# A longer ring of gathered rows, queries kept in DRAM, and buffers that share the ring's place: one graph block on one core

## The chip, the cores and the metric

The kernel runs on one core of one Trainium2 chip. The metric is device time of one launch in microseconds (us). TensorE is the matrix engine (PE in the profile, PEld its weight loads), VectorE is DVE, ScalarE is ACT, GpSimd is POOL, and SyncE is SP; SPq, ACTq and POOLq are the queues on which engines issue DMAs and other instructions that are not counted as busy.

## The reference

One block of a graph network on N = 3125 nodes of D = 256 features with 50000 edges, all in float32. `dst` is sorted and thickest at low node numbers.

```python
dst = (3125 * uniform(50000) ** 2).astype(int)          # sorted; src uniform
xn = layernorm(x)
# 1. graph attention, 8 heads; every node also has an edge to itself
h = einsum('nf,hfd->hnd', xn, W)
e = leaky_relu(a_s[:, src] + a_d[:, dst], 0.2)
alpha = segment_softmax(e, dst)                          # for each head
agg = sum_h softmax(gate)[h] * segment_sum(h[src] * alpha, dst)
g = layernorm(agg + gate @ bias + xn) @ Wo.T + bo
# 2. linear attention over all nodes, 8 heads of 32
q, k, v = rmsnorm(xn) @ w_qkv;  q = elu(q) + 1;  k = elu(k) + 1
o = (q @ (k.T @ v)) / (q @ k.sum(0) + eps)
m = xn + o @ w_out + b_out;  m = m + rmsnorm(m)
x = x + g + m
# 3. mixture of 16 experts, two for each node
x = x + layernorm(xn2 + sum_of_two w_k * expert_k(xn2)),  xn2 = layernorm(x)
```

## The kernel before

The program is four blocks, one after the other; all engines meet between two blocks.

**First stage** (0 to 142 us). Tables for the edges are made, then a software pipeline (`pipeline`, with a lag for each part) goes over NT = 25 tiles of 128 nodes. For tile t, VectorE normalises x; ScalarE copies it to `xna` and copies its transpose (`copies`); TensorE multiplies with w_qkv; ScalarE takes exponentials (`exps`); VectorE forms q and k (`elu`) and writes the source scores `a_s` beside the node's row; TensorE adds k.T v and transposes q; ScalarE copies that transpose to `qT` in SBUF (`qTs`, lag 3, line 393). SP waits for `a_sb` and stores the tile as rows of 272 words in `node_rows` in DRAM (`store`, line 315), and at tiles 7 to 11 also one fifth of `flag_rows` (`store_flags`, line 321). Last it stores `ad_rows` (line 324).

**Edge stage** (142 to 798 us). The 50000 edges, in falling order of `dst`, are cut into 391 chunks of 128; nodes are taken in windows of 16. A step is a chunk met with a window: 592 steps in 37 groups of 16. GpSimd gathers the 128 source rows of each chunk (139 KB) from `node_rows` into a slot of the ring `rows` with an indirect DMA (line 738), in order of chunks:

```python
for k in range(CHUNKS):
    if k >= len(s_rows):                  # FLY = 4 in flight
        landed(k - len(s_rows))           # waits, then raises `fetched`
    if k >= FLY:
        pool.wait_ge(prod.sem, free_at[k])
    pool.indirect_dma_start(rows[:, k % RING, :], ...)
# free_at[k] = max(1, ends[k-FLY] + 2 + AHEAD*G - LEAD,
#                     ends[k-RING] + 2 + AHEAD*G  if k >= RING)
```

`ends[k]` is the last step that uses chunk k, and `prod` counts the products done, from 33 when the first begins. So a gather may start LEAD = 48 steps before the chunk four earlier is used up, and not before the slot's last user is done (RING = 40). For group g, ScalarE waits until `fetched` has reached the group's last chunk and copies the source scores of its 16 steps (`copy_as`, line 917); TensorE turns them to scores (`scores`, line 999) in its turn g + 1, in which it does the products of group g - 1; segment maxima and exponentials follow on VectorE and ScalarE; VectorE spreads the weights over the windows (`spread`, line 819, two of 8 steps) and TensorE multiplies them with the gathered rows (`product`, line 1048) in its turn g + 2. VectorE adds each product to a running sum (`accumulate`, line 835), and SP stores these sums to `agg_rows` in quarters of 8 steps (line 1134).

In the same groups, for g below 25, one tile of linear attention is finished: TensorE multiplies the tile's queries with `kvd` (`num`, line 1058), VectorE adds and inverts the sum (`z_sum`, `z_inverse`) and divides (`divide`), TensorE turns and projects (`turn`, `out_proj`, lines 1065 to 1074). On TensorE `num(0)` stands ahead of group 0's masks, and `out_proj(0)` ahead of `scores(0)`; on VectorE `z_sum`, then `mask_eq` and `bias_parts`, then the inverse, `divide` and `mask_ad`, which needs `adsd`. SP loads `adsd` (line 1123) from `ad_step` before the groups begin, and in them first the flags (line 1127).

**Node stage** (798 to about 1150 us). For each tile the node's own sum is gathered, multiplied with W, added to the residual x2, normalised and sent to its experts' rows.

**Expert stage** (to the end). 64 tiles of 128 rows go through two layers; then each node gathers its two results.

## Time and profile before

| what | value |
|---|---|
| time, median of 3 runs | 1491.21 us (1490.78 to 1492.29) |
| span of the profiled execution | 1489.6 us |
| TensorE busy | 1175.3 us, 79% |
| VectorE busy | 996.3 us, 67% |
| ScalarE busy | 499.2 us, 34% |
| GpSimd busy | 692.2 us, 46% |
| mean granted TensorE clock | 0.887 of 2.4 GHz |
| DMA, mean over the span | 172 GB/s |

Durations below come from the one profiled execution, whose span is 1.6 us below the median of the runs. A granted clock of 1.00 is 2.4 GHz and 0.50 is 1.2 GHz. Busy shares over the whole span mix stages with different limits; the windows by stage are read instead. In a timeline, brackets give how long the engine was idle before the instruction and what released it.

### The profile page before, as it was taken

How to read it: one execution, taken by the hardware profiler on the slowest of the kernel's cores; microseconds unless marked ns; L12 is line 12 of the kernel's file. 1: busy time of each engine (PE TensorE's matmuls, PEld its weight loads, DVE VectorE, ACT ScalarE, POOL GpSimd, SP SyncE). 2: the span in 40 equal slices, each digit the busy share in tenths (PEclk: the TensorE clock that was granted, in tenths of full speed). 3: DMA queues.
4: the chain of work that ended last, by engine and by line, in shares of the span. 5: the costliest groups of instructions: out<-in, count | busy, mean ns of one | idle time of the engine just before them, and what ended most of it. 6: DMA issues, size and time to landing. Idle time of an engine off the chain costs nothing. (4 is left out here: it accounts for less than half of the span.)

```text
span 1489.6 us, 30544 instructions
## 1 busy us (share of the span) xinstructions
PE 1175.3 (79%) x6192; PEld 946.9 (64%) x6193; DVE 996.3 (67%) x2854; ACT 499.2 (34%) x1969; POOL 692.2 (46%) x782
## 2 busy tenths in 40 slices
PE   4996699999999878666672799999991799999900
PEld 4664466666666656444451688888881689999800
DVE  6565388888888867665674588899965234444378
ACT  2453233333333322221121655555521123333301
POOL 1001765666666566666621457676753011111175
PEclk9898599999999998787795799999995799999955
DMA  6062678888888777676757534334413972222155
GB/s 194 30 109 78 142 238 247 238 240 249 249 253 246 234 221 224 207 213 197 222 149 218 195 125 135 127 134 139 143 53 129 343 257 70 70 70 70 61 166 179
DMA packets 219212, 255.70 MB, mean 172 GB/s; under 512 B 57205, under 2 KB 193016, under 8 KB 215640
## 3 DMA queue, kind: packets, MB, share of 16 engines
q1 hardware_dynamic: 177464, 140.79, 30.0%
q0 software_dynamic: 30992, 103.79, 24.1%
q10 hardware_dynamic: 10640, 9.86, 2.1%
q8 instruction: 38, 0.62, 0.2%
q14 instruction: 78, 0.64, 0.1%
HBM read 139.69 MB, written 114.67 MB: 171 GB/s over the span
## 5 line engine op out<-in xcount | busy, mean ns | idle before, releaser
L738 POOL DMA_INDIRECT rows<-node_rows,srcT x391 | 389.0, 995 | 217.5 <-PE pO L1048 107.6
L1048 PE MATMUL pO<-rows,pw 128*128 x1184 | 337.2, 416 | 33.5 <-DVE pw L819 29.4
L835 DVE SCALAR_TENSOR_TENSOR acc<-acc,rsc,pO 128x257 f32<-128x257 f32 x592 | 281.0, 475 | 60.2 <-PE pO L1048 29.9
L1048 PEld LDWEIGHTS pO<-rows,pw 128*128 128x128 f32 x1184 | 216.5, 202 | 78.7 <-issue 51.7
L1408 PE MATMUL pW_<-W_again,aT 128*128 128x256 f32 x800 | 183.1, 383 | 0.4 <-DVE res L1476 0.4
L1408 PEld LDWEIGHTS pW_<-W_again,aT 128*128 128x128 f32 x800 | 149.8, 192 | 19.5 <-DVE res L1476 0.7
L1854 POOL DMA_DIRECT2D ys_rows<-ye x64 | 34.5, 539 | 238.0 <-DVE ye L1805 238.0
L1744 ACT ACTIVATE hT<-pHe,b 128x128 f32<-128x128 f32 x256 | 73.0, 368 | 192.8 <-PE pHe L1770 174.8
L1770 PEld LDWEIGHTS pHe<-xeT,w1e 128*128 128x128 f32 x1024 | 127.4, 196 | 13.7 <-DVE w1e L1795 10.5
L1770 PE MATMUL pHe<-xeT,w1e 128*128 128x128 f32 x1024 | 128.1, 279 | 9.9 <-DVE xeT L1788 9.9
L1779 PE MATMUL pYe<-w,hT 128*128 x512 | 122.1, 382 | 1.2 <-issue 0.6
L1460 DVE SCALAR_TENSOR_TENSOR own<-AG,al,own 128x256 f32<-128x256 f32 x200 | 108.4, 556 | 7.3 <-ACT own L1342 3.6
L917 ACT ACTIVATE asb<-rows 128x8 f32 x592 | 72.9, 209 | 106.2 <-POOLq L729 95.7
L1779 PEld LDWEIGHTS pYe<-w,hT 128*128 128x128 f32 x512 | 92.9, 192 | 12.3 <-issue 2.2
L819 DVE TENSOR_TENSOR pw<-pexp,eq 128x1024 f32<-128x1024 f32 x74 | 87.2, 1220 | 0.0
L1795 DVE COPY w1e<-w 128x1024 f32 x64 | 44.4, 694 | 63.6 <-issue 38.4
L1342 ACT ACTIVATE own<-xna,al 128x256 f32 (+1 forms) x200 | 82.2, 499 | 3.6 <-DVEq L1588 3.6
L1397 PE MATMUL pa<-cst,own 128*128 128x128 f32 x400 | 52.7, 289 | 37.1 <-DVE own L1460 37.1
L1788 DVE COPY xeT<-pXe 128x256 f32<-128x256 f32 x64 | 27.2, 424 | 78.2 <-PE pXe L1760 78.2
L1397 PEld LDWEIGHTS pa<-cst,own 128*128 128x128 f32 x400 | 48.0, 151 | 38.8 <-issue 34.4
L1315 POOL DMA_INDIRECT xs_rows<-ysc,slot_x x50 | 50.9, 1019 | 23.8 <-DVE slot_x L1568 10.3
L1863 POOL DMA_INDIRECT w1e<-ys_rows,slot x50 | 48.8, 976 | 17.2 <-issue 13.4
(332 smaller groups left out, 1929.1 us busy)
## 6 DMA issues: line engine op xcount, KB each, us to landing
agg_rows<-acc SPq DMA_DIRECT2D x296, 256.0 KB
w<-in_ffn_w SPq DMA_DIRECT2D x32, 512.0 KB, 5.8
xe<-xs_rows ACTq DMA_DIRECT2D x64, 128.0 KB, 2.0
ys_rows<-ye POOLq DMA_DIRECT2D x64, 128.0 KB, 2.0
rows<-node_rows,srcT POOLq DMA_INDIRECT x391
node_rows<-xna SPq DMA_DIRECT2D x25, 136.0 KB, 1.8
xna<-in_x SPq DMA_DIRECT2D x5, 640.0 KB, 11.2
mix_rows<-hx SPq DMA_DIRECT2D x25, 128.0 KB
```

The costliest lines, as they stand in the source:

```text
L738: pool.indirect_dma_start(rows[:, k % RING, :], None, node_rows[:, :], at_row(srcT[:, k:k + 1])).then_inc(s_rows[k % len(s_rows)], 16)
L819: dve.tensor_tensor(pw[:, i, :, :].rearrange("p s (d h) -> p s d h", h=H), pexp[:, g % V2, s, :].unsqueeze(2).to_broadcast([P, HG, DW, H]) ...
L835: dve.scalar_tensor_tensor(out=acc[:, k % V3, s % HG, 0:D + 1], in0=before, scalar=rsc[:, g % V2, s:s + 1], in1=pO[n % PB][:, 0:D + 1], op ...
L917: ins = act.activation(asb[:, g % V2, s, :], rows[:, ds(at[s], 1), AS:AS + H].rearrange("p c h -> p (c h)"), ACT.Copy)
L1048: pe.matmul(pO[n % PB][:, 0:D + 1], pw[:, s // HG, s % HG, :], rows[:, ds(at[s % 4], 1), 0:D + 1].rearrange("p c f -> p (c f)"), start=Tru ...
L1342: ins = act.activation(own[:, c, h, :], tile(xna, t, 0, D), ACT.Copy, scale=al[:, 1, t, h:h + 1] if isinstance(t, int) else al[:, 1, ds(t, ...
L1397: mm = pe.transpose(pA[i][:, k * P:(k + 1) * P], own[:, c, n // KD, (n % KD) * P:(n % KD + 1) * P], ident)
L1408: mm = pe.matmul(pW[:, 0:D], aT[:, c, n, :], W[:, n % KD, n // KD, :], start=(n == 0), stop=(n == H * KD - 1))
L1460: ins = dve.scalar_tensor_tensor(out=own[:, c, h, :], in0=AG[:, c, h, :], scalar=al[:, 0, t, h:h + 1] if isinstance(t, int) else al[:, 0, ...
L1744: ins = act.activation(hT[:, c % 2, f, :], pH[c % 2][:, f * P:(f + 1) * P], ACT.Relu, bias=b1[:, ds(e, 1), f:f + 1].rearrange("p e f -> p ...
L1770: mm = pe.matmul(pH[c % 2][:, f * P:(f + 1) * P], w1e[:, c % S3, k, f * P:(f + 1) * P], xeT[:, c % 2, k, :], start=(k == 0), stop=(k == KD ...
L1779: mm = pe.matmul(pY[c % 2][:, 0:D], hT[:, c % 2, f, :], of_expert(w2, e, f), start=(f == 0), stop=(f == FK - 1))
```

## The change

- The ring has 63 slots instead of 40, and a gather may start 96 steps ahead instead of 48.
- Queries of linear attention no longer stay in SBUF. In the first stage ScalarE copies them to one of two buffers `qTo`, after the store of the tile two earlier has landed; SP stores them to DRAM (`store_q`) three turns behind the tile's rows. In the edge stage SP loads tile g + 1 in group g (`load_q`), tile 0 before the groups, and TensorE waits for it in `num`.
- The ring is allocated first and for the whole program. W and WT of the first stage lie in it, and later `y_all`, `x2`, the second W, `b2` and the buffers of the expert stage.
- The semaphores `al_done`, `m_in` and `a_rt` are gone; `al_in` and `al_ex` count on instead.

```diff
-RING, FLY, LEAD, AHEAD = 40, 4, 48, 2
+RING, FLY, LEAD, AHEAD = 63, 4, 96, 2
...
-        both_y = sb("qT_y", [P, NT * D])
-        qT = both_y.rearrange("p (k n) -> p k n", k=KD)
-        y_all = both_y.rearrange("p (t f) -> p t f", f=D)
+        ring = sb("ring", [P, RING * RW])
+        rows = ring.rearrange("p (r f) -> p r f", f=RW)
+
+        def part(lo, *shape):
+
+            n = math.prod(shape)
+            names = "abcd"[:len(shape)]
+            sizes = dict(zip(names, shape))
+            return ring[:, lo:lo + n].rearrange(f"p ({' '.join(names)}) -> p {' '.join(names)}", **sizes)
+
+        Y_END = NT * D
+        y_all = part(0, NT, D)
+        q_rows = dram("q_rows", (NT, P, D))
...
-            W = sb("W", [P, KD, H, D], ctx=ctx)
+            W = part(0, KD, H, D)
...
-            WT = sb("WT", [P, KD, H, KD, P], ctx=ctx)
+            WT = ring[:, KD * H * D:2 * KD * H * D].rearrange("p (k h d n) -> p k h d n", h=H, d=KD, n=P)
+            qTo = sb("qTo", [P, 2, KD, P], ctx=ctx)
+            s_q = [sem(f"s_q{c}") for c in range(2)]
...
-                    pipeline(sp, NT, [(0, store), (0, store_flags)], extra=12)
+                    def store_q(t, c, r):
+                        wait(sp, qT_sb, t)
+                        out_q = q_rows[t, :, :] if isinstance(t, int) else q_rows[ds(t, 1), :, :].rearrange("t p f -> (t p) f")
+                        sp.dma_start(out_q, qTo[:, c, :, :].rearrange("p k f -> p (k f)")).then_inc(s_q[c], 16)
+                    pipeline(sp, NT, [(3, store_q), (0, store), (0, store_flags)], extra=9)
+                    for c in range(2):
+                        sp.wait_ge(s_q[c], 16 * len(range(c, NT, 2)))
                     sp.dma_start(ad_rows.rearrange("(t p) h -> p t h", p=P), ad[:, :, :]).then_inc(moves.sem, 16)
...
                     def qTs(t, c, r):
                         wait(act, qT_ps, t)
-                        act.activation(qT[:, :, t * P:(t + 1) * P] if isinstance(t, int) else qT[:, :, ds(t * P, P)],
-                                       pq[:, 0:D].rearrange("p (k f) -> p k f", k=KD), ACT.Copy).then_inc(qT_sb.sem, 1)
+                        if not isinstance(t, int) or t >= 2:
+                            act.wait_ge(s_q[c], r * 16)
+                        act.sem_inc(s_gate, 1)
+                        act.activation(qTo[:, c, :, :], pq[:, 0:D].rearrange("p (k f) -> p k f", k=KD), ACT.Copy).then_inc(qT_sb.sem, 1)
...
-            rows = sb("rows", [P, RING, RW], ctx=ctx)
+            qTb = sb("qTb", [P, 2, KD, P], ctx=ctx)
+            q_stored = [16 * len(range(c, NT, 2)) for c in range(2)]
...
                     def num(t):
                         wait(pe, mixed, t - 1)
+                        pe.wait_ge(s_q[t % 2], q_stored[t % 2] + 16 * (t // 2 + 1))
                         for g in range(KD):
-                            mm = pe.matmul(pX[:, g * (P + 4):(g + 1) * (P + 4)], qT[:, g, t * P:(t + 1) * P], kvd[:, g, :], start=True, stop=True)
+                            mm = pe.matmul(pX[:, g * (P + 4):(g + 1) * (P + 4)], qTb[:, t % 2, g, :], kvd[:, g, :], start=True, stop=True)
...
-                    groups([(0, load_flags), (2, load_tops), (1, store_x2), (2, store(0)), (1, store_top), (2, store(1))])
+                    def load_q(t):
+                        if t < NT:
+                            wait(sp, num_ps, t - 2)
+                            sp.dma_start(qTb[:, t % 2, :, :].rearrange("p k f -> p (k f)"), q_rows[t, :, :]).then_inc(s_q[t % 2], 16)
+
+                    def load_next_q(g):
+                        load_q(g + 1)
+                    load_q(0)
+                    groups([(0, load_next_q), (0, load_flags), (2, load_tops), (1, store_x2), (2, store(0)), (1, store_top), (2, store(1))])
...
-        W = sb("W_again", [P, KD, H, D], ctx=node_ctx)
-        x2 = sb("x2", [P, NT, D], ctx=node_ctx)
+        x2 = part(Y_END, NT, D)
+        W = part(2 * Y_END, KD, H, D)
...
-                    act.wait_ge(al_done, 1)
+                    act.wait_ge(al_in, 2)
...
-        b2 = sb("b2", [P, E, D], ctx=experts_ctx)
+        b2 = part(Y_END, E, D)
```

## Rows read from the trace of the kernel before

**Rows 1.** Windows: us, busy of PE, PEld, DVE, ACT, POOL; clock, DMA share, GB/s

```profile
210.00:509.00 299.00, 278.72 (x1385) 202.36 (x1384) 256.94 (x702) 105.85 (x600) 185.05 (x183) 1.00 0.82 245
509.00:776.00 267.00, 190.31 (x789) 135.89 (x787) 174.54 (x438) 62.44 (x372) 163.01 (x167) 0.82 0.70 208
```

**Rows 2.** Waits, 509 to 776 us: us in total, times, longest

```profile
ACT asb L917 <- POOLq L729: 65.3, 13, 9.9
...
PE pM L999 <- ACT asb L917: 36.8, 10, 7.3
```

**Rows 3.** Timeline of VectorE, line 819 (start, duration) of groups 1, 21, 35 and 36

```profile
196.14 2.35 DVE L819 TENSOR_TENSOR pw<-pexp,eq 128x1024 f32<-128x1024 f32 x2
...
494.36 2.35 DVE L819 TENSOR_TENSOR pw<-pexp,eq 128x1024 f32<-128x1024 f32 x2
...
761.23 2.35 DVE L819 TENSOR_TENSOR pw<-pexp,eq 128x1024 f32<-128x1024 f32 x2
...
775.07 2.35 DVE L819 TENSOR_TENSOR pw<-pexp,eq 128x1024 f32<-128x1024 f32 x2
```

**Rows 4.** Line 738, whole span: durations, first and last start; its idle time

```profile
L738 POOL DMA_INDIRECT rows<-node_rows,srcT x391: 940/946/1987, 149.3 to 754.6; - x196
...
  PE pO L1048: 107.6, 154
...
  DMA rows<-node_rows,srcT: 23.7, 29
```

**Rows 5.** Window of line 738 alone, its first 45 us: busy, clock, DMA share

```profile
149.00:194.00 45.00, 31.05 (x32) 0.60 0.66 154
```

**Rows 6.** Timeline of ScalarE: the last copy at line 917

```profile
761.68 1.95 ACT L917 ACTIVATE asb<-rows 128x8 f32 x16 [1.64 <-issue]
```

**Rows 7.** Timeline of the first stage, one tile and the next exponential

```profile
60.05 0.69 ACT L378 ACTIVATE ez<-pQ,rr 128x512 f32<-128x512 f32 x1 [1.60 <-PE pV L443]
...
62.56 10.90 SPq L315 DMA_DIRECT2D node_rows<-xna  x4
...
64.66 0.39 ACT L393 ACTIVATE qT_y<-pq 128x256 f32 x1
...
67.10 0.69 ACT L378 ACTIVATE ez<-pQ,rr 128x512 f32<-128x512 f32 x1 [1.46 <-PE pV L443]
```

**Rows 8.** DMA issues: count, KB each, us to landing (6.3: the one at 87.2)

```profile
node_rows<-xna SPq DMA_DIRECT2D x25, 136.0 KB, 1.8
...
flag_rows<-flags SPq DMA_DIRECT2D x5, 516.0 KB, 6.7
...
adsd<-ad_step SPq DMA_DIRECT2D x1, 320.0 KB, 9.8
...
ad_rows<-ad SPq DMA_DIRECT2D x1, 100.0 KB, 4.2
...
node_rows<-xna SPq DMA_DIRECT2D x1, 136.0 KB, 6.3
```

**Rows 9.** A window of 1 us of TensorE, right behind an idle stretch

```profile
134.00:135.00 1.00, 1.00 (x6) 0.50 0.40 139
```

**Rows 10.** Timeline, the end of the first stage

```profile
134.72 0.38 ACT L393 ACTIVATE qT_y<-pq 128x256 f32<-128x256 f32 x1 [2.33 <-PE pq L458]
...
140.96 0.83 DVE L621 SCALAR_TENSOR_TENSOR stepT<-stepT,firstT 128x640 f32<-128x640 f32 x1
```

**Rows 11.** Timeline, the start of the edge stage

```profile
150.07 1.22 PE L1058 MATMUL pMix<-kvd,qT_y 128*128 128x132 f32 x4 [12.03 <-DMA mix_bo<-in_mix_b_out]
...
154.98 8.45 SPq L1127 DMA_DIRECT2D flg<-flag_rows  x2
...
162.19 1.22 PE L1074 MATMUL pMix<-xna,cst 128*128 128x256 f32 x2
...
164.35 0.29 DVE L762 TENSOR_TENSOR adb<-cst,adsd 128x128 f32<-128x128 f32 x1 [6.53 <-DMA adsd<-ad_step]
...
166.74 0.77 PE L999 MATMUL pM<-cst,asb 128*128 128x128 f32 x2 [3.33 <-ACT asb L917]
```

More of the change, by code:

```diff
@@ L18 @@
+import math
 from contextlib import ExitStack
@@ L1173, in build @@
             md_win = dram("md_win", (2 * P * DW, 2 * H))
-            s_mdw, al_in, al_ex, al_done, scale_in = sem("s_mdw"), sem("al_in"), sem("al_ex"), sem("al_done"), sem("scale_in")
+            s_mdw, al_in, al_ex, scale_in = sem("s_mdw"), sem("al_in"), sem("al_ex"), sem("scale_in")
             lr = sb("lr", [P, 2], U32, ctx)
@@ L1185, in build @@
             te = sb("te", [P, 3, E], ctx=ctx)
-            a_rt, m_in, free_in, zero_in = sem("a_rt"), sem("m_in"), sem("free_in"), sem("zero_in")
+            free_in, zero_in = sem("free_in"), sem("zero_in")
             cleared = sem("b2_in")
@@ L1383, in _ @@
                     clear(act, 1)
-                    act.wait_ge(m_in, 1)
-                    act.activation(m[:, 0, :], m[:, 0, :], ACT.Exp).then_inc(a_rt, 1)
+                    act.wait_ge(al_in, 3)
+                    act.activation(m[:, 0, :], m[:, 0, :], ACT.Exp).then_inc(al_ex, 1)
                 @block.tensor
@@ L1587, in _ @@
                         line.do(dve.tensor_tensor(al[:, i, :, :], es[:, 1, :, :], es[:, 2 + i, :, :], ALU.mult))
-                    dve.sem_inc(al_done, 1)
+                    dve.sem_inc(al_in, 1)
                     PICK, L = [(7, top(i)) for i in range(10)], [(8, place(i)) for i in range(5)]
@@ L1626, in _ @@
                     line.do(dve.tensor_scalar(slot[:, :, :].rearrange("p k t -> p t k"), sy[:, :, :], float(SLOTS - 1), None, ALU.min))
-                    dve.tensor_tensor(m[:, 0, :], picks[:, :, 2 * E + 3], picks[:, :, 2 * E + 2], ALU.subtract).then_inc(m_in, 1)
-                    dve.wait_ge(a_rt, 1)
+                    dve.tensor_tensor(m[:, 0, :], picks[:, :, 2 * E + 3], picks[:, :, 2 * E + 2], ALU.subtract).then_inc(al_in, 1)
+                    dve.wait_ge(al_ex, 2)
                     line.do(dve.tensor_scalar(m[:, 1, :], m[:, 0, :], 1.0, None, ALU.add))
@@ L1649, in build @@
             S3 = 3
-            xe = sb("xe", [P, S3, D], ctx=ctx)
-            xeT = sb("xeT", [P, 2, KD, P], ctx=ctx)
-            w1e = sb("w1e", [P, S3, KD, F], ctx=ctx)
-            hT = sb("hT", [P, 2, FK, P], ctx=ctx)
-            ye = sb("ye", [P, 2, D], ctx=ctx)
+            at = Y_END + E * D
+            w1e = part(at, S3, KD, F)
+            at += S3 * KD * F
+            hT = part(at, 2, FK, P)
+            at += 2 * FK * P
+            xe = part(at, S3, D)
+            at += S3 * D
+            xeT = part(at, 2, KD, P)
+            at += 2 * KD * P
+            ye = part(at, 2, D)
+            at += 2 * D
+            xb = part(at, 2, D)
             pX = [ps(ctx, f"pXe{c}") for c in range(2)]
@@ L1678, in build @@
             g = flat_w1[:, 0:VU * 2 * D].rearrange("p (u k f) -> p u k f", k=2, f=D)
-            xb = sb("xb", [P, 2, D], ctx=ctx)
             v = flat_w1[:, VU * 2 * D:VU * 3 * D].rearrange("p (u f) -> p u f", f=D)
```

## The prediction

> **What bounds the kernel now.** I read the windows by stage first. From 210 to 509 us TensorE is busy 279 of 299 us at full clock; from 509 to 776 us it is busy only 190 of 267 us, DMA is less used than before, and the mean granted clock is 0.82 [rows 1]. The reader is to see that the edge stage falls into two halves, and that the second is short of something. The waits of that half say of what: ScalarE waits 65.3 us at line 917 for GpSimd's count of landed gathers, and TensorE then waits 36.8 us for that copy [rows 2]. The timeline of VectorE's line 819, which opens each of the 37 groups, gives the pace: groups 1 to 21 take (494.36 - 196.14)/20 = 14.91 us each. At that pace group 36 would open 15 groups later at 718; it opens at 775.07. The last two groups, for which all rows were there, are 13.84 us apart, since the node work in the group (25 tiles) is over [rows 3].
>
> Is it the gathers' own speed, or when they may start? GpSimd's row answers: 391 gathers from 149.3 to 754.6, at least 0.94 us each, and 154 of them waited for a matmul at line 1048, 107.6 us in all [rows 4]. That is free_at: 48 steps ahead, or slot free. In the first half a chunk is used for nearly 2 steps (windows are met along with chunks), so 48 steps are some 27 chunks; toward the end a chunk lasts 1 step (0.93 us) and a gather takes longer than that. What GpSimd stood still for in the first half is missing in the second. Of 48 steps some 30 are needed anyway, because the copy at line 917 runs two groups ahead of the products.
>
> **The ring (63 slots, 96 steps).** A wait that is met at once still shows 0.3 us of idleness, so the true wait is 107.6 - 154 x 0.3 = 61.4 us [rows 4]. Would the new bounds hold a gather? From the formula of dst, chunk k ends near step s(k) = k + 195 (1 - (1 - k/391)^2). With the chain going on at 1.4 us a gather, gather 184 starts 258 us after the first, and its step bound, s(180) - 96 = 222 steps of 0.93 us after products begin at 181 (one group before 196.14), is passed 20 us earlier; gather 243 needs slot s(180) = 318, passed 12 us earlier; gather 390 needs s(327) = 517, over 25 us earlier. So the waits on products vanish and the chain lasts 605.3 - 61.4 = 543.9 us, 1.395 us a gather. The first 45 us, in which no bound holds it, show the same: 32 gathers, 1.41 us each [rows 5].
>
> Against that, waits for landings (only four gathers may be in flight) partly hid behind the waits on products, and DMA, at a share of 0.82 in the first half [rows 1], carries a tenth more a microsecond. Bounds: nothing added (1.395), or 1.50 a gather, at which two thirds of the gain is gone. The rows are nearer to the first (the second half, short of gathers, is less loaded than the first), so I take 12 us, 0.03 a gather. Removed: 61.4 - 12 = 49.4 us. The last copy began 7 us after the last gather started, held by ScalarE's order and not by the landing [rows 6]; now it follows the landing by perhaps 5 us, 2 us more. From the copy to group 36's opening is 13.4 us as now [rows 3, 6]. Everything from there to the end is unchanged in work.
>
> The Trainium skill (DMA: Bandwidth & Descriptors, Queues, rings and completion order) says that each DMA engine takes packets from its queue rows in turn. By it the gathers, on a row of their own, would not slow with SP's load, and the 12 us would be nought. No row of before shows the chain free and the load full at once.
>
> **Queries stored (first stage).** Per tile SP issues one more DMA (25 of 128 KB), and ScalarE, before it copies tile t's queries, waits for the store of t - 2. SP gets to store_q(t) only after store(t + 2). The loop turns in 3.52 us. From the exponential at 60.05 to SP's issue of that tile's rows is 2.51 us; from the query copy at 64.66 to the next exponential 2.44 us, of which 1.46 idle, so 0.98 of work [rows 7]. Two tiles, 7.04 us, must hold 2.51 + 0.4 (SP's issue) + landing + 0.1 + 0.98, so the landing may take 3.0 us. Node rows, 136 KB, take 1.8 us [rows 8]: hidden, with 1.2 us left. If that cover goes, each microsecond above 3.0 costs one per two tiles.
>
> It goes at tiles 7 to 11, where SP also stores the flags: 516 KB in small packets, 6.7 us to land, and node rows issued 3 us behind one take 6.3 us, so the queue is served in order [rows 8]. The query store comes right behind: a landing 0.4 + 6.7 + 0.8 after SP's store, a two-tile cycle of 2.51 + 7.9 + 0.1 + 0.98 = 11.5 instead of 7.04. Queued behind the waiting ScalarE copy are the next tile's x copies and exponentials, for which VectorE and TensorE wait. Five flag stores stand in three such cycles: 3 x 4.4 = 13 us. Slower tiles thin the backlog (less, 9), and a TensorE that has stood idle comes back at half clock [rows 9] (more, up to 18). I take 13. The other end is nought, if ScalarE had as much air as it has elsewhere; the rows for the flags exclude it.
>
> At the stage's end ad_rows now follows the last query store: the copy at 134.72 + 0.38, SP 0.1, 1.8 to land, ad_rows 4.2 to land [rows 8]: 141.2, and VectorE works until 141.8 [rows 10]. Nothing, or 0.5 us if it fails.
>
> **Queries loaded (edge stage).** 25 loads, each a group ahead of its use: hidden by a 15 us group. Not the first. load_q(0) stands on SP behind adsd, which takes 9.8 us to land [rows 8]; SP's next two issues there took 8.45 us, so the queue is full. VectorE sees adsd at 164.35; the queries land near 165.2 instead of being in place at 150.07. The line-1058 matmul, z_sum, the bias work, division and projection take 150.07 to 163.41, which adsd covered; all of it moves by 15.1 us, to 178.5, and the scores of group 0 behind it on TensorE from 166.74 to 178.5: 11.8 us [rows 11]. Who is late? Products, not gathers, and the gathers are what sets the end. So I cost it at nothing, covered by the gather chain; uncovered it is 11.8 us.
>
> **Layout and semaphores.** W, WT, y_all, x2, b2 and the expert buffers lie in the ring, al_done, m_in and a_rt are merged into counters in the same order: same instructions, same order, nothing. A buffer's address costs nothing that a row shows.
>
> **Sum.** 1489.6 + 13 - 49.4 - 2 = 1451.2; the runs' median lies 1.6 above the profiled 1489.6, so 1452.8, 1453.
>
> **Check from the consumer.** Without lack of rows group 36 opens at 494.36 + 3 x 14.91 + 12 x 13.84 = 705, plus 13 and 11.8: 730. The sum has it at 775.1 - 38.4 = 736.7. The gathers still bound, by 7 us only, so cheaper gathers can give no more than 7 us beyond the sum.
>
> **Rivals.** (a) The consumer bounds: gathers at 1.395 or less, or the flag slips nearer to 9. Both together give 1442. For it: the two clocks of the check lie close. Chance 0.17. (b) Gathers slow under load to about 1.48: 0.055 x 390 = 21 us more than mine, 1474. For it, the landing waits that were hidden; against it, the first 45 us. Chance 0.15. (c) Slower than before: the wait at landed(k - 4), with four in flight, takes the place of the wait for products. Each gather at g gives a sum of 1453 + 390 (g - 1.426); it decides from g = 1.53, where a landing would take 4 x 1.53 = 6.1 us on average. At 1.60 the time is 1521. Rows show only 29 such waits among 391, none on the average gather. Chance 0.10. (d) The change of the ring does nothing, because gathers are bound by DMA anyway: then only 13 us are added, 1504. Against it the 61.4 us of waits on products, which are no DMA. Chance 0.03. (e) About no change, between (b) and (c): 0.03. My forecast has 0.52.
>
> **Range.** 1438 takes in (a) with the flags at 9 and VectorE's tail groups faster than 13.84; 1486 takes in (b) with flags at 18 and part of (e). Beyond lie (c) and (d). Measurement can tell 0.2% (3 us) from no change. Faster 0.84, same 0.03, slower 0.13.
>
> **What would show it.** Right: GpSimd's waits on line 1048 nearly gone, last gather about 36 us earlier, no wait of ScalarE at line 917 before 600 us; group 36 opening near 737; a gap of TensorE of some 4 us three times between 75 and 105 us; line 1058 first at 165 plus the first stage's delay. Wrong: landing waits on most gathers; ScalarE waiting on stores in every tile of the first stage; SP's stores of acc late enough that VectorE waits for them.

## The result, and the profile after

The changed kernel takes 1497.89 us (median of 9 runs, 1492.69 to 1501.47), the kernel before 1491.62 us on the same chip (median of 9 runs, 1488.63 to 1493.55 but for one odd run of 2627.41 us). The ratio of the fast runs is 1.0043, 95% interval 1.0026 to 1.0060: slower by 0.4%, where 1453 us was forecast. The profiled execution has a span of 1495.9 us, 6.3 us above that of before. The sum had 38.4 us below it.

Windows of the two halves of the edge stage, columns as in [rows 1]:

```profile
210.00:509.00 299.00, 279.22 (x1382) 200.76 (x1381) 256.33 (x701) 106.02 (x600) 186.61 (x184) 1.00 0.84 255
509.00:776.00 267.00, 194.88 (x867) 141.17 (x865) 186.47 (x472) 67.72 (x401) 170.37 (x168) 0.87 0.73 216
```

The gather line over the whole span (least, median and longest duration in ns, first and last start), and what its engine sat idle for, as [rows 4]:

```profile
L760 POOL DMA_INDIRECT ring<-node_rows,srcT x391: 940/946/1968, 156.6 to 759.8; - x196
its engine sat idle before it (us, times) until:
  PE pO L1070: 91.9, 130
  issue: 91.0, 222
  DMA ring<-node_rows,srcT: 25.4, 36
```

Waits of 509 to 776 us, as [rows 2], and the timeline of `spread` for groups 0, 1, 21 and 36, as [rows 3]:

```profile
ACT asb L939 <- POOLq L751: 56.8, 13, 10.9
...
PE pM L1021 <- ACT asb L939: 32.3, 8, 8.3
```

```profile
193.86 1.21 DVE L841 TENSOR_TENSOR pw<-pexp,eq 128x1024 f32<-128x1024 f32 x1
...
214.67 1.22 DVE L841 TENSOR_TENSOR pw<-pexp,eq 128x1024 f32<-128x1024 f32 x1
...
513.71 1.22 DVE L841 TENSOR_TENSOR pw<-pexp,eq 128x1024 f32<-128x1024 f32 x1
...
779.88 1.22 DVE L841 TENSOR_TENSOR pw<-pexp,eq 128x1024 f32<-128x1024 f32 x1
```

The picture of before stands almost unchanged. GpSimd still shows 130 waits for the product's matmul, 91.9 us of them (154 and 107.6 before), ScalarE still waits 56.8 us for gathered rows in the second half, and the groups still keep 14.95 us and then slow down. The gathers take (759.8 - 156.6)/390 = 1.547 us each, 1.552 before. They start 7.25 us later, their chain is 2.1 us shorter, group 36 opens 20.1 us behind the last of them instead of 20.5, and the rest of the kernel takes 716.0 us instead of 714.5: 7.25 - 2.1 - 0.4 + 1.5 = 6.3 us, the whole difference of the two spans. The question is why the waits on products are still there.

The query parts are visible too. Timeline of ScalarE's query copy, and the two matmuls that answer to [rows 11]:

```profile
77.52 0.38 ACT L415 ACTIVATE qTo<-pq 128x256 f32<-128x256 f32 x1 [4.84 <-issue]
...
87.94 0.38 ACT L415 ACTIVATE qTo<-pq 128x256 f32<-128x256 f32 x1 [4.74 <-issue]
...
98.38 0.39 ACT L415 ACTIVATE qTo<-pq 128x256 f32<-128x256 f32 x1 [4.72 <-issue]
```

```profile
172.13 1.25 PE L1081 MATMUL pMix<-kvd,qTb 128*128 128x132 f32 x4 [27.60 <-DMA qTb<-q_rows]
...
185.51 0.64 PE L1021 MATMUL pM<-cst,asb 128*128 128x128 f32 x2
```

Three waits of 4.7 to 4.8 us stand where three of 4.4 were predicted. The first node tile's product comes 22.06 us later and group 0's scores 18.77 us later, of which 7.25 are the first stage's.

### The profile page after: what moved, and what is told of

The parts are those of the page before. It is cut to its first block and busy times, and to the rows that moved or that the text cites. A ratio compares the mean times of both kernels' runs of the same rounds, so it can differ in the third digit from the quotient of the medians.

```text
span 1495.9 us, 30670 instructions
## 1 busy us (share of the span) xinstructions
PE 1163.6 (78%) x6192; PEld 937.2 (63%) x6193; DVE 999.9 (67%) x2854; ACT 501.6 (34%) x1969; POOL 697.6 (47%) x782
## 5 line engine op out<-in xcount | busy, mean ns | idle before, releaser
L760 POOL DMA_INDIRECT ring<-node_rows,srcT x391 | 395.2, 1011 | 209.3 <-PE pO L1070 91.9
L1070 PE MATMUL pO<-ring,pw 128*128 x1184 | 329.9, 408 | 33.8 <-DVE pw L841 29.5
L1070 PEld LDWEIGHTS pO<-ring,pw 128*128 128x128 f32 x1184 | 211.1, 198 | 80.1 <-issue 56.4
L1439 PE MATMUL pW_<-ring,aT 128*128 128x256 f32 x800 | 181.6, 380 | 0.4 <-DVE res L1507 0.4
L1439 PEld LDWEIGHTS pW_<-ring,aT 128*128 128x128 f32 x800 | 148.9, 191 | 18.8 <-DVE res L1507 0.5
L1781 ACT ACTIVATE ring<-pHe,b 128x128 f32<-128x128 f32 x256 | 73.2, 368 | 194.6 <-PE pHe L1807 194.6
L1807 PEld LDWEIGHTS pHe<-ring 128*128 128x128 f32 x1024 | 127.5, 196 | 12.7 <-DVE ring L1832 9.5
L1807 PE MATMUL pHe<-ring 128*128 128x128 f32 x1024 | 128.3, 280 | 8.8 <-DVE ring L1825 8.8
L1816 PE MATMUL pYe<-w,ring 128*128 x512 | 122.2, 382 | 1.8 <-issue 1.2
L1816 PEld LDWEIGHTS pYe<-w,ring 128*128 128x128 f32 x512 | 92.9, 191 | 13.2 <-issue 3.1
```

Source lines behind the costliest of these rows:

```text
L760: pool.indirect_dma_start(rows[:, k % RING, :], None, node_rows[:, :], at_row(srcT[:, k:k + 1])).then_inc(s_rows[k % len(s_rows)], 16)
L1070: pe.matmul(pO[n % PB][:, 0:D + 1], pw[:, s // HG, s % HG, :], rows[:, ds(at[s % 4], 1), 0:D + 1].rearrange("p c f -> p (c f)"), start=Tru ...
L1439: mm = pe.matmul(pW[:, 0:D], aT[:, c, n, :], W[:, n % KD, n // KD, :], start=(n == 0), stop=(n == H * KD - 1))
L1781: ins = act.activation(hT[:, c % 2, f, :], pH[c % 2][:, f * P:(f + 1) * P], ACT.Relu, bias=b1[:, ds(e, 1), f:f + 1].rearrange("p e f -> p ...
L1807: mm = pe.matmul(pH[c % 2][:, f * P:(f + 1) * P], w1e[:, c % S3, k, f * P:(f + 1) * P], xeT[:, c % 2, k, :], start=(k == 0), stop=(k == KD ...
L1816: mm = pe.matmul(pY[c % 2][:, 0:D], hT[:, c % 2, f, :], of_expert(w2, e, f), start=(f == 0), stop=(f == FK - 1))
```

## What GpSimd does between two gathers

A wait's releaser in the profile is inferred. So I looked at GpSimd's own records between gathers. Before each one it has five: the increment behind the landing wait (line 751), the read of `free_at[k]` from SBUF into a register (line 757), a register operation and a check on its range, and the increment behind the wait on products (line 759). Here are four gathers, the reads in the same stretch, and the reads of the whole stage after and before (least, median, longest in ns):

```profile
309.03 0.94 POOL L760 DMA_INDIRECT ring<-node_rows,srcT  x1 [1.17 <-PE pO L1070]
310.28 0.94 POOL L760 DMA_INDIRECT ring<-node_rows,srcT  x1 [0.31 <-issue]
312.70 0.94 POOL L760 DMA_INDIRECT ring<-node_rows,srcT  x1 [1.48 <-PE pO L1070]
314.27 0.94 POOL L760 DMA_INDIRECT ring<-node_rows,srcT  x1 [0.63 <-PE pO L1070]
```

```profile
L757 POOLq TENSOR_LOAD <-free_at x1: 323/323/323, 308.9 to 308.9; - x1
...
L757 POOLq TENSOR_LOAD <-free_at x1: 739/739/739, 310.9 to 310.9; - x1
...
L757 POOLq TENSOR_LOAD <-free_at x1: 642/642/642, 312.6 to 312.6; - x1
...
L757 POOLq TENSOR_LOAD <-free_at x387: 283/298/1180, 159.4 to 758.0; - x194
```

```profile
L735 POOLq TENSOR_LOAD <-free_at x387: 282/296/1297, 152.2 to 753.0; - x194
```

The gather at 312.70 had a read of 739 ns ahead of it, and before that read the landing's increment came 0.75 us later than at the least. The profile wrote the gather's 1.48 us down to the product. The gather at 314.27 had a read of 642 ns, and its 0.63 us are written down to the product too. GpSimd's queue works off increment, read, wait and issue in order. With a read of 283 ns that takes 1.21 us at the least, which just fits the 1.25 us of one gather and its gap of 0.31 us. What a read takes beyond that is lost. Adding up GpSimd's records over all gathers gives, in us:

```
                                        before   changed   e14 (queries alone)
from range check to increment, over      17.9      2.0       32.1   true wait on products
  its least 0.06 (waits on products)
reads of free_at over 0.283              59.0     61.8       62.1
from there to the next landing's         54.5     65.4       52.9   issue of the gather
  increment, over its least 0.57                                    and wait for a landing
steps of gathers over 1.25, summed      117.8    115.8      133.5
```

The first three rows add up to the chain: 386 cycles of the queue's least 1.21 us and the three terms give 599, 597 and 615 us, and from the first landing's increment to the 387th the queue took 600.8, 598.6 and 616.4 us. So it is GpSimd's queue that sets the pace of the gathers.

The same records say what stood behind the product's name. In the kernel before, the 154 gathers written down to the product had 59.9 us of idleness above 0.31 us each. Ahead of them lie 15.1 us of true waits on products, 31.7 us of reads over 0.283 and 26.2 us of issue and landing waits (73.0 us in all, more than the idleness, since the queue runs a little ahead of the gathers and takes some of them up). In the changed kernel the 130 such gathers had 51.6 us: no true wait, 28.4 us of reads and 31.5 us of issue and landing waits.

There is a second way to the true waits: `free_at` worked out from dst, against the starts of the product matmuls. In the kernel before, 27 gathers, between gather 52 and gather 107, start at most 1.55 us after the matmul that frees them starts (the least is 1.2 us), with 13.4 us of idleness above 0.3 us each. In the changed kernel every gather starts at least 27 us after that matmul. So the new bounds held nothing there, and the waits written down to products are about half reads and half issue and landing waits.

## The experiments

Sixteen runs were made. The first four ran on a chip on which the kernel is slower (the kernel before takes 1571.02 us there, and groups 1 to 21 of e1 to e4 take 17.1 to 18.1 us each instead of 14.9), so they compare with the kernel before on that chip alone. e5 to e8 share a second chip, e9 to e12 a third, e13 to e16 a fourth. "Held" counts gathers that start at most 1.55 us after the start of the product that frees them, and gives their idleness in us above 0.3 us each.

| run | median us | ratio to before, 95% | first, last gather | us a gather | held | group 36 |
|---|---|---|---|---|---|---|
| e1 | 1597.45 | 1.0117 (1.0069 to 1.0165) | 158.0, 843.1 | 1.757 | 87, 76.9 | 872.3 |
| e2 | 1602.37 | 1.0158 (1.0084 to 1.0233) | 160.1, 818.2 | 1.687 | 79, 59.4 | 872.6 |
| e3 | 1577.19 | 1.0013 (0.9975 to 1.0052) | 149.3, 820.0 | 1.720 | 87, 75.5 | 848.8 |
| e4 | 1600.37 | 1.0155 (1.0081 to 1.0228) | 157.6, 817.9 | 1.693 | 91, 64.4 | 871.9 |
| e5 | 1471.70 | 0.9855 (0.9821 to 0.9889) | 157.2, 733.3 | 1.477 | 0 | 756.1 |
| e6 | 1650.49 | 1.1040 (1.1004 to 1.1077) | 160.7, 918.4 | 1.943 | 0 | 937.0 |
| e7 | 1478.61 | 0.9888 (0.9848 to 0.9929) | 149.4, 739.0 | 1.512 | 27, 39.4 | 761.8 |
| e8 | 1503.41 | 1.0065 (1.0043 to 1.0087) | 162.4, 765.2 | 1.546 | 0 | 785.7 |
| e9 | 1473.93 | 0.9886 (0.9812 to 0.9960) | 157.1, 733.9 | 1.479 | 0 | 754.9 |
| e10 | 1494.00 | 1.0000 (0.9976 to 1.0024) | 150.4, 759.4 | 1.561 | 0 | 782.2 |
| e11 | 1466.65 | 0.9821 (0.9786 to 0.9856) | 159.0, 707.9 | 1.408 | 39, 35.7 | 750.9 |
| e12 | 1453.79 | 0.9741 (0.9704 to 0.9777) | 149.1, 702.9 | 1.420 | 22, 42.8 | 738.5 |
| e13 | 1501.21 | 1.0066 (1.0040 to 1.0091) | 155.2, 763.7 | 1.560 | 0 | 786.9 |
| e14 | 1516.85 | 1.0158 (1.0127 to 1.0190) | 158.8, 779.8 | 1.592 | 43, 26.4 | 802.5 |
| e15 | 1440.68 | 0.9649 (0.9613 to 0.9686) | 147.1, 688.2 | 1.388 | 22, 34.3 | 722.8 |
| e16 | 1456.28 | 0.9770 (0.9735 to 0.9805) | 147.0, 713.3 | 1.452 | 52, 55.5 | 738.1 |

**e1, queries alone.** The changed kernel with the old bounds (its layout of buffers stays too).

```diff
-RING, FLY, LEAD, AHEAD = 63, 4, 96, 2
+RING, FLY, LEAD, AHEAD = 40, 4, 48, 2
```

> The changed kernel with the modulus of the ring back at 40 slots and the step bound back at 48; queries still go through DRAM. Theory A (the ring brings nothing, since gathers are paced by their landings; the cost is that of the stored queries in the first stage, 7 to 10 us, less what slack hides): 1495 to 1501 us, the same as the changed kernel within 3 us, last gather near 760. Rival B (the ring did bring something and the queries cost more than they show): clearly slower than the changed kernel, 1505 us or more, last gather 770 or later.

**e2 and e3, eight in flight**, in the changed kernel and in the one before (there 40, 4, 48 become 40, 8, 48).

```diff
-RING, FLY, LEAD, AHEAD = 63, 4, 96, 2
+RING, FLY, LEAD, AHEAD = 63, 8, 96, 2
```

> The changed kernel with FLY = 8 gathers in flight instead of 4 (later counts reuse other semaphores, which changes no work). Theory A1 (four in flight is what paces the gathers: each takes 6 us and more to land under load, so 1.55 us a gather): gathers come down to 1.30 to 1.42 us each, the last one starts at 665 to 710, the time falls to 1440 to 1465 us. Rival A2 (the DMA engines or GpSimd's own queue are used up, and more in flight only wait longer): 1.50 to 1.55 us each, 1490 to 1500 us.

> The kernel before with FLY = 8 instead of 4; ring of 40 and step bound of 48, which now looks at the chunk eight earlier, so it is some 6 steps looser. If the step bound and the landings pace the gathers by turns: faster than before by 8 to 25 us, 1466 to 1483 us. If the landings alone do: as much faster as eight in flight makes the changed kernel. If neither: within 3 us of before.

**e4, half the stores.** The changed kernel, whose edge stage leaves out half of each sum when it stores it (and the node stage reads half back).

```diff
-                                             acc[:, k % V3, q * HP:(q + 1) * HP, 0:D]).then_inc(s_agg[k % V3], 16)
+                                             acc[:, k % V3, q * HP:(q + 1) * HP, 0:D // 2]).then_inc(s_agg[k % V3], 16)
```

> The changed kernel, which leaves out the upper half of the features when it stores the running sums and reads them back (the lower half stands in for it). Edge stage DMA falls by about a quarter; four gathers in flight as in the changed kernel. Theory A (landings of gathers are long because the DMA engines also carry the stores): gathers at 1.30 to 1.40 us each, last gather at 665 to 705, 1440 to 1465 us. Rival (a gather takes long to land by itself, or GpSimd's issue paces it): 1.50 us or more each, last gather after 740, 1485 us or more.

e1 and e3 say that queries alone cost 1.2% there and eight in flight in the old kernel nothing. In e2 no wait of a gather is written down to a landing. In e4 the DMA share of 210 to 509 us is 0.60, against 0.74 in e2:

```profile
210.00:509.00 299.00, 247.13 (x1144) 175.81 (x1142) 213.38 (x586) 88.44 (x487) 175.09 (x176) 0.94 0.74 220
```

```profile
210.00:509.00 299.00, 246.04 (x1113) 176.58 (x1113) 209.24 (x571) 85.74 (x480) 169.95 (x172) 0.92 0.60 159
```

Yet the times are 1602.37 and 1600.37, and e1, with four in flight, the old bounds and all stores, takes 1597.45. The changed kernel as it is was not run on that chip, so what either edit gives against it is not measured; neither gave what its theory asked for. Later the table's column "held" offered a reason: on that chip the groups are so slow that products hold 79 to 91 gathers, with the long ring too. So these runs do not settle what four in flight or the DMA load cost on the other chips. e4 is worth most for the reads. They last 410 ns on the mean in e1 and in e2, and 319 ns in e4, and 42 of e2's reads last over 0.7 us against 4 of e4's; over the reads of e2 and e4 that is 48.7 and 14.0 us above 283 ns each. The read is longer when more is stored.

**e5, one read and one wait for four gathers; e6, seven increments more before each gather; e7, e5's edit in the kernel before; e8, the changed kernel again**, all on one chip. My theory then was the supply of instructions to GpSimd's queue, since the long gaps stood at the same gathers in every run.

```diff
-                        if k >= FLY:
-                            steps = pool.value_load(free_at[0:1, k:k + 1], ...)
+                        if k >= FLY and k % 4 == 0:
+                            last = min(k + 3, CHUNKS - 1)
+                            steps = pool.value_load(free_at[0:1, last:last + 1], ...)
                             pool.wait_ge(prod.sem, steps)
                             pool.sem_inc(s_gate, 1)
```

> The changed kernel, with the bound on free slots read and waited on once for four gathers (for the last of the four), so that GpSimd executes some 3.25 recorded instructions a gather instead of some 7. Theory (the unrolled instruction stream of GpSimd pauses for more instructions every some 64 of them, and these pauses are what the gathers lose over their bare 1.25 us): the pauses come every some 20 gathers instead of every 9, a gather costs 1.35 to 1.42 us, the last gather starts at 690 to 715 us instead of 760, and the kernel is 2 to 3% faster than the one before. Rival 1 (the gathers have a pace of their own, by descriptors or the data they move): 1.50 us or more a gather, time within 5 us of the changed kernel without this edit. Rival 2 (the step bound was the wait after all, the queries having delayed the consumer): the wait for the last of four is later by three gathers each time, so the gathers are no quicker and the time 0 to 10 us longer.

```diff
+                        for _ in range(7):
+                            pool.sem_inc(s_gate, 1)
                         pool.indirect_dma_start(rows[:, k % RING, :], ...)
```

> The changed kernel with seven idle increments of a semaphore on GpSimd ahead of each gather, so twice the recorded instructions. Their bare cost is some 0.35 us a gather (0.05 us each), which alone gives 1.60 to 1.70 us a gather and 20 to 60 us on the time; that is what the rival expects (no pauses for instructions). Theory: besides that the pauses come every 4 to 5 gathers instead of every 9, a gather costs 1.9 to 2.2 us and the time rises by 130 to 250 us.

> The kernel before with the same edit as the one above (one wait on the products for four gathers), ring of 40 slots and lead of 48 kept. Theory: with fewer instructions the gathers could go at 1.35 to 1.42 us, and then the step bound of the short ring ends the waits: the gathers follow the products, one per 1.45 to 1.55 us, and the kernel gains 0.3 to 1.5% over before; the ring of 63 in the run above gains more than that. Rival (the ring is never the bound): the old ring gains as much as the new one or more, by the 6 to 13 us which the queries cost.

> The changed kernel as it is, on the chip of the three above, to compare them with: 0 to 1% slower than the kernel before, 1.50 to 1.60 us a gather if the chip is like the first, 1.65 to 1.75 if it is like that of the first four runs.

Gather lines of e5 and of e6:

```profile
L761 POOL DMA_INDIRECT ring<-node_rows,srcT x391: 940/946/2005, 157.2 to 733.3; - x196
its engine sat idle before it (us, times) until:
  issue: 86.9, 264
  DMA ring<-node_rows,srcT: 56.7, 82
  PE pO L1071: 38.6, 44
```

```profile
L762 POOL DMA_INDIRECT ring<-node_rows,srcT x391: 940/944/1981, 160.7 to 918.4; - x196
its engine sat idle before it (us, times) until:
  PE pO L1072: 184.8, 191
  issue: 170.6, 187
```

e5 ends 31.7 us sooner than e8 on the same chip, by an edit that makes its waits stricter. Its time fits neither number: 1.477 us a gather, where the theory wanted 1.35 to 1.42 and the rival 1.50. e6 decides. Its 1.943 lies inside the theory's range, but for another reason: the median step of its gathers is 1.78 us, the queue's records of the seven increments stand 78 ns apart (0.55 us in all, not 0.35), and steps over 0.6 us above the median number 23, against 67 in the changed kernel. With twice the instructions the pauses must have become more frequent. They became rarer, and the theory of instruction supply fell. It is then that I added up the reads. e7 shows the bound of the short ring once it really holds: waits at gathers 28, 32, 36 and so on, 39.4 us.

**e9, the read once for four, the wait before each.** Against e5 it puts back the wait and the increment before each gather, but not the three other reads. With each of these goes its register operation and its range check.

```diff
                         if k >= FLY:
+                            if k % 4 == 0:
+                                last = min(k + 3, CHUNKS - 1)
+                                steps = pool.value_load(free_at[0:1, last:last + 1], ...)
                             pool.wait_ge(prod.sem, steps)
```

> The changed kernel, with the bound read from free_at once for four gathers (the bound of the last of the four), but GpSimd waits on it and increments s_gate before each gather as before. In the changed kernel the 387 reads at line 757 last 283 ns at the least and 443 ns on the mean, 62 us in all above their least, and the 391 gathers start 116 us later in all than at 1.25 us each. Theory (the latency of that read is what stood in the profile as waits on products, and it lies bare in GpSimd's queue): the pace is that of the run with one wait for four, 1.46 to 1.49 us a gather, last gather at 730 to 740, time 1466 to 1478 us. Rival (it is the number of instructions or the wait itself): 1.53 us or more a gather, time above 1490 us.

1.479 us a gather and 1473.93 us (four runs, 1465.76 to 1487.62): e5's pace (1.477), as the theory of the reads had it, and far from the rival's 1.53. The reads over 283 ns sum to 17.5 us instead of 61.8. The chain of gathers is 576.8 us instead of 603.2, so the reads with their register work are worth 26.4 us of it; e9 does not tell their excess over 283 ns from their fixed part. The releaser is still written down as the product in 99 cases, though no product holds a gather (the nearest is 10.7 us off):

```profile
L762 POOL DMA_INDIRECT ring<-node_rows,srcT x391: 940/946/2003, 157.1 to 733.9; - x196
its engine sat idle before it (us, times) until:
  issue: 77.9, 225
  PE pO L1072: 65.7, 99
  DMA ring<-node_rows,srcT: 44.2, 63
```

**e10, query stores issued by ScalarE**, right behind its copy, instead of by SP behind the flags.

```diff
-                    pipeline(sp, NT, [(3, store_q), (0, store), (0, store_flags)], extra=9)
+                    pipeline(sp, NT, [(0, store), (0, store_flags)], extra=12)
...
                         act.activation(qTo[:, c, :, :], ...).then_inc(qT_sb.sem, 1)
+                        wait(act, qT_sb, t)
...
+                        act.dma_start(out_q, qTo[:, c, :, :].rearrange("p k f -> p (k f)")).then_inc(s_q[c], 16)
```

> The changed kernel, with the 25 stores of queries issued by ScalarE right behind its copy, and so not behind the node rows and flags on SyncE's queue. Theory (7.25 us of the first stage's length are query stores queued behind the flag stores): the waits of 4.7 us at the query copy are gone, the first gather starts at 149 to 152 us, and the time falls by 4 to 7 us from the changed kernel's, all of it in the start of the gathers; that the first node tile's product comes earlier changes nothing. Rival (the copy itself and ScalarE's order make the stage longer, or the landing is slow wherever it is issued): the first gather at 155 us or later and under 2 us of gain.

The first gather starts at 150.4, 6.1 us sooner, and the waits of 4.7 us are gone, so the stores' place on SP behind the flags was the slip. The ratio falls from 1.0043 and 1.0065 to 1.0000, 6 to 10 us, across chips. In the profiled execution (1498.36, the upper end of ten), the slower pace of 1.561 takes the gain back; the time is thus carried by the runs and not by that trace.

**e11, read for four and eight in flight; e12, read for eight, eight in flight and e10's edit.**

```diff
-RING, FLY, LEAD, AHEAD = 63, 4, 96, 2
+RING, FLY, LEAD, AHEAD = 63, 8, 96, 2
...
-                        if k >= FLY:
+                        if k >= FLY and k % 8 == 0:      # 4 in e11
+                            last = min(k + 7, CHUNKS - 1)
```

> The changed kernel, with one read and one wait for four gathers and eight gathers in flight instead of four. With four in flight that pace was 1.477 us a gather and 20 to 33 waits for a landing took 57 us of idle time (32 us above the 0.3 us that every gather shows). Theory (after the read the next limit is the four in flight): no waits for landings, 1.39 to 1.44 us a gather, last gather at 700 to 720, time 1445 to 1460 us. Rival (the gathers then only queue up in the DMA engines, and the wait comes back as late landings at ScalarE's copy, or the idle time stays under another name): 1.46 us or more, time 1465 us or more.

> All together: one read and one wait for eight gathers, eight in flight, queries stored by ScalarE. Theory: the first gather at 149 to 152 us, 1.36 to 1.42 us a gather, last gather at 685 to 705; from there the consumer (group 36 not before some 730 us at its own pace) begins to set the end, so the time is 1433 to 1450 us. Rival (the longer reach of the wait, up to eight gathers, meets the bound of 96 steps): waits on products at every eighth gather in the first third, 1.45 us or more a gather, 1455 us or more.

The gathers do what was expected (708 and 703), the times do not: 1466.65 and 1453.79, above both ranges. e11's chain is 548.9 us, 27 us shorter than e5's with four in flight (across chips), so the four in flight were worth about as much as the reads; the idleness written down to landings falls from 56.7 us in 82 waits to 6.1 in 20. Group 36 opens 43 and 36 us after the last gather, 20 in the changed kernel. Now the consumer sets the end, and the bound of the long ring holds gathers, from gather 108 in e11 and from 96 in e12.

```profile
L761 POOL DMA_INDIRECT ring<-node_rows,srcT x391: 940/946/2003, 159.0 to 707.9; - x196
its engine sat idle before it (us, times) until:
  issue: 102.7, 325
  PE pO L1071: 47.4, 43
  DMA ring<-node_rows,srcT: 6.1, 20
```

**e13, the first query load ahead of adsd, in the changed kernel; e14, e1 again on a chip of usual speed; e15, e12 with e13's edit; e16, the kernel before with e11's two edits.**

```diff
+                    sp.dma_start(qTb[:, 0, :, :].rearrange("p k f -> p (k f)"), q_rows[0, :, :]).then_inc(s_q[0], 16)
                     sp.wait_ge(s_gad, 16 * SJ)
...
-                    load_q(0)
```

> The changed kernel, with the load of the first query tile issued ahead of adsd and so not behind its 10 us. Theory (the gathers set the end, and the consumer has room at the start): group 0 opens some 10 us earlier, at 183 to 186 instead of 193.9, the gathers keep their pace, and the time stays within 2 us of the changed kernel's, 1.003 to 1.007 of the kernel before. Rival (the late start of the products costs something, by the bound of 96 steps or by the groups behind it): 4 us or more of gain, a ratio of 1.002 or less.

> The changed kernel with the bounds of the kernel before (40 slots, 48 steps), so the queries through DRAM alone. Theory: in the kernel before the bounds held 27 gathers for 13 us in all, between gathers 52 and 107; with the products starting 11.5 us later still they hold more of them, for some 20 to 30 us. So queries alone give 7 us by the later first gather and 5 to 12 us by the bound: 1.008 to 1.013 of the kernel before, and the new bounds take back 6 to 12 us of it in the changed kernel. Rival (the ring brings nothing at all): the same time as the changed kernel, 1.004 to 1.0065.

> The run with all three edits (read for eight, eight in flight, queries stored by ScalarE; 1453.8 us), and the load of the first query tile ahead of adsd. There the last gather started 35.6 us ahead of the opening of group 36 instead of 20, so the consumer set the end. Theory (the consumer's later start is then on the path): group 0 opens 8 to 11 us earlier and the whole is 5 to 11 us faster, 1443 to 1449 us. Rival (the gathers are bound again as soon as the consumer is earlier, since both are close): 0 to 4 us, 1450 us or more.

> The kernel before, with one read and one wait for four gathers and eight in flight, ring of 40 slots and 48 steps kept. The changed kernel with the same two edits took 1466.7 us. Theory (with the reads out of the way the short bounds are the limit): waits on products at nearly every fourth gather up to some 200, 1.49 to 1.53 us a gather, 1472 to 1480 us, as with four in flight (1478.6), so the longer ring is worth 5 to 13 us there, its queries' cost included. Rival (the ring is worth nothing even then): 1460 us or less, by the 7 us that the queries cost.

e13: group 0 opens at 181.3 instead of 193.9, and the time stays (1.0066). The consumer's late start cost nothing, as predicted. e14: queries alone cost 1.6%, more than my 0.8 to 1.3%; the last gather is 25.2 us later than in the kernel before, 9.5 by the start and 15.7 by the pace. 43 gathers are held, now from gather 28 on. The changed kernel's last gather is 20.0 us sooner than e14's, and e13's, on e14's chip, 16.1: that is what the ring brings. e15: with the consumer at the end, the same edit as e13's is worth 13 us (1453.79 to 1440.68, across chips), more than expected; it is 3.5% faster than the kernel before. e16: my expectation failed. 52 gathers are held for 55.5 us, as I had said, but the time is 1456.28, as the rival had it (1460 or less) and 10 us below e11 with the long ring (across chips). Its group 0 opens at 173.0 and e11's at 197.4, and group 36 at 738.1 against 750.9: with reads out of the way the consumer's start counts for more than the ring. That is read from two traces and not varied alone. Against e15, on the same chip, which has both late starts mended (and one read for eight), e16 is 15.6 us slower.

## Why the prediction was wrong, point by point

- **The failed step: "So the waits on products vanish and the chain lasts 605.3 - 61.4 = 543.9 us".** I took the releaser's name for the cause. Ahead of those 154 gathers the queue's records show 15.1 us of waits on products (17.9 over all gathers), 31.7 us of long reads of `free_at` and 26.2 us of waits for issue and landing. Only the first went; the other two stayed. The same formula gives 91.9 - 130 x 0.3 = 52.9 us for the changed kernel, in which no gather waited for a product. The chain lasted 603.2 us. One read for four brings it to 576.8 (e9), and eight in flight besides to 548.9 (e11): near 543.9 only when both are gone. The check that I had, 32 gathers at 1.41 us with no bound in force [rows 5], pointed the same way: that stretch has a DMA share of 0.66, and its reads are shorter (49 ns above 283 on the mean up to 194 us, 166 from 210 to 509). I read it as the pace without bounds, but it was the pace at less load too.
- **The bounds.** The prediction found them passed 20, 12 and over 25 us earlier, with products at 181 us, and did not set its own 11.8 us of later products against that. In the changed kernel steps 222 and 318 are done at 408 and 497 us, so at the 1.395 us a gather of the sum gather 243 would have been held some 5 us, and at 1.426 it would have had 2.5 us to spare. The 27 us that it had were owed to the slow pace; at 1.41 (e11) the long ring's bounds held 39 gathers for 35.7 us.
- **The 12 us for load on landings.** Issue of the gather and landing waits grew from 54.5 to 65.4 us, 10.9. 15.9 us less waiting on products, 2.8 more in reads and 10.9 more here leave 2.2 us, and the gathers' chain is 2.1 us shorter (605.3 to 603.2). The size was right and the saving that it was set against was not. Part of it is the hiding that the prediction named: with 32.1, 17.9 and 2.0 us of true product waits (e14, before, changed) issue and landing take 52.9, 54.5 and 65.4. The Trainium skill (DMA: Bandwidth & Descriptors, Queues, rings and completion order) says that each DMA engine takes packets from its rows in turn. That gathers would then not slow was my inference, and no run here shows their landings under two loads with all else equal.
- **The first stage, 13 us.** The mechanism was right: three waits of 4.7 us behind the flags, gone in e10. The stage is 7.25 us longer, not 13. The loop stood about 2.7 us ahead of before when it came to the flags (the first flag store at 70.8 us instead of 73.5), so the slip itself is some 10.
- **Consumer's start.** num(0) 14.8 us later net of the stage (15.1 predicted), scores 11.5 (11.8), at no cost (e13). Right, and right too that it costs once the cover is gone: e15.
- **2 us at the end, layout and semaphores at nothing.** From the last gather to group 36's opening 20.1 us, 20.5 before; from there to the end 716 us, 714.5 before. Nothing to see beyond scatter.
- **Check from the consumer.** 13.84 us a group for the tail was too short: in e15, where ScalarE waits only 8.4 us for gathered rows from 600 us on, groups 28 to 36 take (722.8 - 600.4)/8 = 15.3 us. The 13.84 came from the last step alone, and the last step takes 13.85 in e15 too.
- **Rivals.** (c), slower than before, comes nearest by its number: its sum gives 1453 + 390 x (1.547 - 1.426) = 1500 us for the pace measured. By its mechanism it was half right: landing waits did stay in the chain, but only 36 gathers were written down to them, and its rows had no long reads. (d), "the change of the ring does nothing", 1504 us, is near for a wrong reason (DMA as the bound) and with 13 for the queries. In fact the queries with the new layout cost some 25 us in the old ring (e14), and the ring brings 14 to 20.

Open: what in the stores slows the read (port, queue or fabric); what eight in flight alone gives on a chip of usual speed, since e2 ran where products hold the gathers; what a read costs by its excess over 283 ns alone; and why e4's shorter reads left its time within 2 us of e2's. The held gathers of that chip would explain the last, but e4 was not run on another.

## What to carry to other kernels

The name beside an idle time is that of the last semaphore in line and need not be the cause: before costing a wait as gone, work out when its condition was met, and add up the engine's uncounted instructions between two of its busy ones. A wait that is taken away also uncovers what was hidden beneath it, so look for the next one (here the landings) before the gain is booked. In a loop that its issuing queue paces, a word read into a register before each transfer is a cost of its own; read it once for four and wait for the last. And where two chains run close (gathers and their consumer here), what an edit is worth depends on which is ahead: the same earlier query load gave 0 us and 13 us.

## What the runs showed of the hardware

A read of one word from SBUF into a GpSimd register takes 283 ns at the least and up to 1.2 us in the changed kernel (1.3 in the one before), 443 ns on the mean. It is longer with more stores in flight: 410 ns on the mean in e2 and 319 in e4, which stores half. An increment of a semaphore costs GpSimd's queue 0.078 us (e6).

A gather's own 0.94 us becomes up to 1.97 us. All 21 gathers of the changed kernel above 1.5 us start while VectorE's pair of multiplies at line 841 runs, whose two operands are both in SBUF. The 62 gathers that start in such a pair take 1.30 us on the mean, the others 0.96:

```profile
364.33 1.93 POOL L760 DMA_INDIRECT ring<-node_rows,srcT  x1 [0.30 <-issue]
...
395.29 1.96 POOL L760 DMA_INDIRECT ring<-node_rows,srcT  x1 [0.30 <-issue]
```

```profile
394.06 2.37 DVE L841 TENSOR_TENSOR pw<-pexp,eq 128x1024 f32<-128x1024 f32 x2
```

Over 391 gathers of 1011 ns on the mean instead of 940 that is 28 us of GpSimd's time. The Trainium skill (Advanced Engine Details and Errata, GPSIMD Details) says that GpSimd shares a read and a write interface with VectorE and meets it in instructions with two SBUF inputs; the rows agree. No run here moves the multiply, so what it costs the kernel is not shown; the sum of the queue's terms above, which comes within 2 us without it, leaves it little.
